# Float16 products, rows turned by DMA and three dense experts in a mixture-of-experts layer behind attention

## What is computed

```python
w, idx = _gate(xf, wg)
fe = idx.reshape(-1)
oh = jax.nn.one_hot(fe, E, dtype=jnp.int32)
pos = (jnp.cumsum(oh, axis=0) * oh).sum(-1) - 1
keep = pos < cap
dest = jnp.where(keep, fe * cap + pos, E * cap)
...
xe = xp[buf_tok].reshape(E, cap, DIM)
h = jax.nn.silu(jnp.einsum('ecd,edh->ech', xe, w1)) * jnp.einsum('ecd,edh->ech', xe, w3)
out = jnp.einsum('ech,ehd->ecd', h, w2) * buf_w.reshape(E, cap, 1)
y = jnp.zeros((N + 1, DIM), x.dtype).at[buf_tok].add(out.reshape(E * cap, DIM))[:N]
z = jax.nn.silu(xf @ sw1) * (xf @ sw3) @ sw2
return (y + z).reshape(shape)
```

## Time and profile before

| | |
|---|---|
| median of 3 runs | 969.25 us (966.09 to 976.89) |
| span of the profiled execution | 977.5 us |
| TensorE, VectorE, ScalarE, GpSimd busy | 859.0, 654.3, 616.8, 673.5 us |
| mean granted clock of TensorE | 0.943 of full speed |

### The profile page before, as it was taken

The page is one execution under the profiler, slowest core; times in us unless marked ns, Lnnn a source line. Parts: engine busy times, 40 slices in busy tenths (PEclk is TensorE's granted clock), DMA queues, the critical chain, the costliest instruction groups (busy, mean ns, idle before and its releaser), DMA issues. The chain is left out here.

```text
span 977.5 us, 25690 instructions
## 1 busy us (share of the span) xinstructions
PE 859.0 (88%) x9439; PEld 633.9 (65%) x9439; DVE 654.3 (67%) x2448; ACT 616.8 (63%) x1189; POOL 673.5 (69%) x580
## 2 busy tenths in 40 slices
PE   5789999999999999999999999766688888888654
PEld 2367777777777777777777777654465666666422
DVE  7757788987987987987987986836243434343217
ACT  3668889888888888888898787733132323233305
POOL 7656665699698699699689689346665555556636
PEclk9989999999999999999999999978798989899968
DMA  5787788645444454354354342016333323333147
GB/s 160 182 255 234 231 243 220 177 107 134 97 119 111 101 135 108 89 151 107 73 141 122 72 117 64 21 51 197 119 96 100 96 79 95 95 101 99 39 191 252
DMA packets 104428, 126.62 MB, mean 130 GB/s; under 512 B 22077, under 2 KB 65426, under 8 KB 103408
## 3 DMA queue, kind: packets, MB, share of 16 engines
q1 hardware_dynamic: 95408, 109.25, 40.8%
q0 software_dynamic: 8896, 15.74, 5.2%
HBM read 33.68 MB, written 41.58 MB: 77 GB/s over the span
## 5 line engine op out<-in xcount | busy, mean ns | idle before, releaser
L2289 POOL TENSOR_TENSOR PL<-PF,PH 128x1280 f16<-128x1280 f32 x121 | 317.8, 2626 | 107.2 <-ACT PH L1632 63.7
L1854 DVE CUSTOM_DVE_ANT_0 JUNK<-PS,M 128x256 f16<-128x256 f32 (+3 forms) x512 | 225.2, 485 | 39.5 <-PE PS L1265 35.8
L1626 ACT ACTIVATE PF<-PS 128x512 f32<-128x512 f32 (+1 forms) x384 | 192.8, 520 | 80.3 <-PE PS L1298 75.4
L2332 POOL DMA_INDIRECT y_rows<-BIG,Q x150 | 145.7, 972 | 99.3 <-ACT BIG L1551 57.4
L1632 ACT ACTIVATE PH<-PF 128x1280 f16<-128x1280 f32 x128 | 162.2, 1267 | 0.6
L2322 POOL DMA_INDIRECT xe_rows<-PAY,DEST x128 | 129.3, 1010 | 42.9 <-issue 27.7
L1291 PE MATMUL PS<-Q,K 128*128 128x512 f16 (+3 forms) x512 | 148.6, 300 | 9.2 <-DMA Q<-MROW 4.9
L1315 PE MATMUL PS<-VH,PH 128*128 128x65 f16 x1280 | 141.3, 195 | 13.0 <-DVE Y L1896 8.5
L1317 PE MATMUL PS<-VH,PL 128*128 128x65 f16 x1280 | 141.3, 194 | 1.2 <-issue 1.2
L1315 PEld LDWEIGHTS PS<-VH,PH 128*128 128x128 f16 x1280 | 119.6, 98 | 35.0 <-issue 24.5
L1316 PE MATMUL PS<-VL,PH 128*128 128x64 f16 x1280 | 141.3, 194 | 0.0
(11 more groups left out here) (252 smaller groups left out, 2027.5 us busy)
## 6 DMA issues: line engine op xcount, KB each, us to landing
K<-KH SPq DMA_DIRECT2D x128, 128.0 KB, 2.3
Q<-QH SPq DMA_DIRECT2D x128, 128.0 KB, 2.4
xe_rows<-PAY SPq DMA_DIRECT2D x20, 520.0 KB, 4.2
Q<-xe_rows SPq DMA_DIRECT2D x30, 325.0 KB
K<-KL SPq DMA_DIRECT2D x64, 128.0 KB, 2.3
Q<-QL SPq DMA_DIRECT2D x64, 128.0 KB, 2.3
y_rows<-PAY SPq DMA_DIRECT2D x16, 512.0 KB, 4.9
K<-in_L_ffn_w_dram SPq DMA_DIRECT2D x96, 64.0 KB
```

The lines of the kernel that those rows point to most:

```text
L1626: e.activation(PF[:, n % PBUF, c0:c0 + width], PS[:, k, 0:width], ACT.Exp).then_inc(s["c_exp"], 1)
L1854: e.tensor_tensor_reduce(JUNK[:, n_ttr % 2, 0:width], PS[:, base + ab, c0:c0 + width], M0[:, 512 - width:512], 1.0, -3e38, ALU.add, ALU.ma ...
L2289: e.tensor_tensor(PL[:, n % PBUF, :], PF[:, n % PBUF, :], PH[:, n % PBUF, :], ALU.subtract).then_inc(s["c_lp"], 1)
L2332: e.indirect_dma_start(out=y4[:, :], out_offset=bass.IndirectOffsetOnAxis(ap=XE[:, x_ % 6, k, 128:129].bitcast(I32), axis=0), in_=OUT[:, x ...
```

## The change

What it does, part by part:

- **Float16 products.** The first layers' operands, rows and weights w1 and w3, are split into a high float16 half (ScalarE) and a low one (VectorE: value less high half), and a product is high x high + high x low + low x high. The second layers stay float32.
- **Rows turned by DMA.** TensorE's turns and their copies go. SyncE issues a DMA transpose of 128 x 1280 float16 for each expert (both halves of its 640 rows) and one of 128 x 1024 for each batch of x1. The stores of the turned x1 to DRAM and their loads go. `xe_rows` is read so that each partition takes five rows that lie 128 apart, not five neighbours.
- **Three dense experts**, four early ones: 29 gathered experts, not 30, and 36 dense pieces (8 shared, 24, 4).
- **TensorE's order**: a front group is the second layer of expert x with the first of x + 2, then a dense group, the second layer of one piece with the first layer of the next; periods 1 to 3 have two dense groups. A group tells the other engines of its end once, behind its last product. Silu and times stand ahead of the five copies.
- Loads of weight sets and of the early experts' rows stand at the end of the attention part in SyncE's order; the last unit's and batch 7's PSUM banks are assigned anew (6 for one half, 7 for the other).

The diff, cut to its core:

```diff
-ND = 2
+ND = 3
 NE = E - ND
-NA = 2
-NS1 = 5
-TAIL = 2
+NA = 4
 SHARED = -1
-DENSE = ([(SHARED, b) for b in range(NS1, NB)] + [(d, b) for d in range(ND) for b in range(NB)]
+DENSE = ([(SHARED, b) for b in range(NB)] + [(d, b) for d in range(ND) for b in range(NB)]
          + [(ND + j, NB - 1) for j in range(NA)])
...
 WEIGHTS = list(range(ND + NA))
...
+SPLITS = [0, SHARED, *range(1, NA + ND)]
...
+    def group(*work):
+
+        told = c["c_pe"].up()
+        for k, (name, a) in enumerate(work):
+            step(name, a, k == len(work) - 1)
+            marks[name, a] = told
+
+    def rows_out(x_):
+        for k in range(5):
+            step("rows out", x_, k)
+
+    begun = []
+
+    def front(*work):
+
+        group(*work)
+        for name, a in reversed(work):
+            if name == "hidden":
+                step("silu", a)
+                step("times", a)
+            else:
+                step("outs", a)
+
+    def dense():
+        nonlocal piece
+
+        work, ended, upped = [], begun[:], None
+        if begun:
+            work.append(("dense down", begun.pop()))
+        if piece < len(DENSE):
+            upped = piece
+            work.append(("dense up", piece))
+            begun.append(piece)
+            piece += 1
+        group(*work)
+        if upped is not None:
+            step("dense silu", upped)
+            step("dense times", upped)
+        for i in ended:
+            step("dense add", i)
...
+        if ms == NH - 3:
+            for j in range(NA + ND):
+                step("load set", j)
+            for x_ in range(NA, NA + 4):
+                step("load ring", x_)
+            for x_ in range(NA):
+                step("load rows", x_)
...
+    rows_in(1)
+    step("set split", SHARED)
+    x1_in(0)
+    piece = 0
+    front(("hidden", 0))
+    step("set split", 1)
+    x1_in(1)
+    rows_in(2)
+    dense()
...
+    front(("product", 0), ("hidden", 1))
+    rows_out(0)
+    step("load rows", 4)
+    step("set split", 2)
+    x1_in(2)
+    rows_in(3)
+    dense()
+    front(("hidden", 2))
+    step("set split", 3)
+    x1_in(3)
+    x1_in(4)
+    dense()
+    splits = SPLITS[5:]
+    forms = list(range(len(WEIGHTS)))
+    for x_ in range(1, NE):
+        rows_in(x_ + 3)
+        if NA <= x_ + 3 < NE:
+            step("ring split", x_ + 3)
+        if x_ + 4 < NE:
+            step("load rows", x_ + 4)
+        if x_ + 2 < NE:
+            front(("product", x_), ("hidden", x_ + 2))
+        else:
+            front(("product", x_))
+        rows_out(x_)
+        if NA + 4 <= x_ + 4 < NE:
+            step("load ring", x_ + 4)
+        dense()
+        for b in (3 + 2 * x_, 4 + 2 * x_):
+            if 5 <= b < NB:
+                x1_in(b)
+        for k in forms[0:2]:
+            step("form", k)
+        forms = forms[2:]
+        for j in splits[0:1]:
+            step("set split", j)
+        splits = splits[1:]
+        if x_ <= 3:
+            dense()
+    while piece < len(DENSE):
+        dense()
+    dense()
+    return steps, marks, {name: x.sem for name, x in c.items()}
...
+        def three(out, halves, m, x_of, free):
+
+            high, low = halves[:, 0, 128 * m:128 * m + 128], halves[:, 1, 128 * m:128 * m + 128]
+            for o, n in free:
+                e.matmul(out(o, n), high, x_of(0, o, n), start=True, stop=False)
+                e.matmul(out(o, n), high, x_of(1, o, n), start=False, stop=False)
+            for o, n in free:
+                i = e.matmul(out(o, n), low, x_of(0, o, n), start=False, stop=True)
+            return i
...
+            three(lambda o, n: PSF[:, o:o + n], halves, 0, rows, ((512, 128),))
+            three(lambda o, n: PSF[:, 896 + o:896 + o + n], halves, 1, rows, ((0, 128),))
+            three(lambda o, n: PSF[:, o:o + n], halves, 0, rows, ((0, 512),))
+            i = three(lambda o, n: PSF[:, 896 + o:896 + o + n], halves, 1, rows, ((128, 512),))
+            if tell:
+                i.then_inc(s["c_pe"], 1)
...
+        def dense_down(i, tell):
+
+            d, b = DENSE[i]
+            if d == SHARED:
+                w.wait_ge(l_sw, 48)
+            else:
+                w.wait_ge(l_set[set_of(d)], 48)
+            w.wait_ge(s_dh, i + 1)
+            w.wait_ge(s_dacc, i)
+            for q in range(4):
+                p = e.matmul(PS[:, 7, q * 128:(q + 1) * 128], DH[:, i % 2, q * 128:(q + 1) * 128], down_weights(d),
+                             start=True, stop=True)
+            if tell:
+                p.then_inc(s["c_pe"], 1)
...
+            elif name == "rows split":
+                x_, = a
+                w.wait_ge(l_xe[x_ % 6], 16 * (x_ // 6 + 1))
+                w.wait_ge(l_xt[(x_ - 2) % 3] if x_ >= 2 else None, 16 * ((x_ - 2) // 3 + 1))
+                for key in unit_done(LAST):
+                    w.wait_ge(*at(*key))
+                e.activation(XS16[:, x_ % 2, 0, :].rearrange("p (k n) -> p k n", k=5), XE[:, x_ % 6, :, 0:128],
+                             ACT.Copy).then_inc(s_rh, 1)
...
+            elif name == "rows split":
+                x_, = a
+                w.wait_ge(s_rh, x_ + 1)
+                w.wait_ge(l_xe[x_ % 6], 16 * (x_ // 6 + 1))
+                w.wait_ge(l_xt[(x_ - 2) % 3] if x_ >= 2 else None, 16 * ((x_ - 2) // 3 + 1))
+                e.tensor_tensor(XS16[:, x_ % 2, 1, :].rearrange("p (k n) -> p k n", k=5), XE[:, x_ % 6, :, 0:128],
+                                XS16[:, x_ % 2, 0, :].rearrange("p (k n) -> p k n", k=5), ALU.subtract).then_inc(s_rl, 1)
...
+        def load_ring(x_):
+            r = x_ - NA
+            if r < 4:
+                for key in unit_done(LAST - 1):
+                    w.wait_ge(*at(*key))
+            else:
+                w.wait_ge(*at("product", x_ - 4))
             for m, src in enumerate((w1, w3, w2)):
-                e.dma_start(EW[:, x_ % 4, m, :], src[expert(x_)]).then_inc(l_w[x_ % 4], 16)
+                e.dma_start(EW[:, r % 4, m, :], src[expert(x_)]).then_inc(l_w[r % 4], 16)
 
         def load_rows(x_):
             b = NB - 1 if x_ >= NA else NB - 2
+            for key in unit_done(LAST - 1 if x_ < 4 else LAST):
+                w.wait_ge(*at(*key))
             w.wait_ge(*at("scat", b, 0))
             w.wait_ge(*at("scat", b, 1))
-            w.wait_ge(s_ys[(x_ - 6) % 4], 80 * ((x_ - 6) // 4 + 1))
-            w.wait_ge(s_turn, x_ - 5)
-            w.wait_ge(s_oc, 5 * (x_ - 5))
+            w.wait_ge(s_ys[(x_ - 6) % 4], 80 * ((x_ - 6) // 4 + 1) if x_ >= 6 else 0)
             e.dma_start(XE[:, x_ % 6, :, :], xe_e[expert(x_)]).then_inc(l_xe[x_ % 6], 16)
...
+            elif name == "rows split":
+                x_, = a
+                w.wait_ge(s_rh, x_ + 1)
+                w.wait_ge(s_rl, x_ + 1)
+                w.wait_ge(*at("pv", NH - 1))
+                w.wait_ge(*at("hidden", x_ - 3))
+                e.dma_start_transpose(XT[:, x_ % 3, :, :].rearrange("p w (k r) -> p (w k) r", r=128),
+                                      XS16[:, x_ % 2, :, :].rearrange("p w n -> p (w n)")).then_inc(l_xt[x_ % 3], 16)
```

More of the change, by code:

```diff
@@ L510, in finish @@
         part("pick", 1)
-        if not whole:
-            unlock((f"pick {half[0]}", b))
         yield
@@ L546, in last_unit @@
         yield
-        step("first out", pj_free[0])
+        step("first out")
         mark("wo", u, "first", by="c_pm")
@@ L562, in last_unit @@
         for half in (0, 1):
-            step("last out", half, (pj_free[1], (("xa", u, "first"),))[half])
+            step("last out", half)
             mark("wo", u, half, by="c_pm")
@@ L773, in plan @@
         scatter()
-    for b in range(NB - 1):
-        load_x1t(b)
-    for e_ in range(4):
-        load_w(e_)
-    step("load dense")
-    for x_ in range(NA):
-        step("load early rows", x_)
-    gate_free = (st_free[0], st_free[1])
     halves = [finish(NB - 1, 0), finish(NB - 1, 1)]
@@ L805, in plan @@
     upto(1, "payi")
-    parts = [shared(b) for b in range(NS1)]
     for half, gen in enumerate(halves):
@@ L813, in plan @@
         if half == 0:
-            next(parts[0])
-            next(parts[1])
+            step("set split", 0)
+            rows_in(0)
     for _ in last:
         pass
-    load_x1t(NB - 1)
-    for b in range(2):
-        next(parts[b])
-    for b in range(2):
-        next(parts[b])
-        next(parts[b])
-    step("early turn", 0)
-    next(parts[2])
-    next(parts[2])
-    step("early hidden", 0)
-    step("early turn", 1)
-    next(parts[3])
-    next(parts[3])
-    step("early product", 0)
@@ L1462, in tensor @@
+            elif name == "hidden":
                 hidden(*a)
-            elif name == "early product":
+            elif name == "product":
                 product(*a)
-        def weights(d, m):
-            return SW[:, m, :] if d == SHARED else DW[:, d, m, :] if d < ND else AW[:, d - ND, m, :]
-        def dense_up(i):
-            d, b = DENSE[i]
-            one, two = (2, 3) if i >= IN_LOOP and i % 2 else (0, 1)
```

(11 more changed lines are left out.)

683 lines of the change are left out of this document (301 added, 382 removed).

## The result

The changed kernel took **988.31 us** (median of 4 runs, 982.30 to 993.46) beside 967.67 for the kernel before (4 runs, 964.04 to 976.89): a ratio of 1.0174, 95% interval 1.0101 to 1.0247. It is 1.7% slower; 922 was predicted. The profiled execution lasted 991.7 us beside before's 977.5; that is 14.2 us between the traces, against 20.6 between the medians, since before's profiled execution lies beside the slowest of its four.

What follows compares the result with a forecast made beforehand. GpSimd waiting behind TensorE bounded the loop; afterwards GpSimd would. Expert 4 at 733.7, last scatter 891.9, loads 894.1, plus 36.3 gives 930.4 instead of 977.5; 47 off the median 969.25 makes 922 us, range 910 to 936.

Steps and rivals of the forecast that it cites:

- GpSimd stood still for 50 us behind TensorE: Expert loop before: 149 scatter steps of 1.276 would be 190.1 us but took 240.6; the difference was winnable.
- TensorE's period of 6.75 us: Old expert loop: turns, dense and expert layers sum to 6.75 us at full clock, 0.37 above GpSimd's 6.38.
- TensorE's new period, 4.99: Expert loop after: float16 first layers 1.62 and 1.26, second layers 1.11 and 1.00, no turns: 4.99 us.
- the loop of buffers: Row load, splits, transpose and first layer take 14 us against three experts' 19.1: five us of slack, hidden.
- the buffer loop is too long: Rival, expert loop: contention makes load and transpose take over 5.1 us more; 15 to 40 us, 937 to 962; chance 0.08.
- GpSimd the bound at 6.38: Expert loop after: five scatters of 1.276 us set 6.38 us an expert, above TensorE's 5.6 at the old clock.
- The start: First experts: GpSimd idles 4 us, three periods of about 10.4 us follow, expert 4's scatters start at 733.7.
- The end: After the last scatter: landing 2.2 us, dense pieces lose 2, earlier sums gain 2; y_rows loads at 894.1.
- scatters slowed by VectorE: Rival, expert loop: VectorE splits with two SBUF inputs hold scatters; 29 us, 951, or half, 937; chance 0.12.
- the row I went by: Earlier trace: scatter at 674.20 beside VectorE's L2078, both inputs in SBUF, still takes 0.97 us; spoke against slowed scatters.
- TensorE at half clock: Rival, expert loop: idle gaps lower TensorE's clock; at 0.50 the period is 10.0 us, total 1,012; chance 0.04.

Runs made afterwards that it cites:

- the first comparison: The changed kernel against the kernel before, without further edits: 988.31 us beside 967.67, ratio 1.0174.
- sets 1, 2 and 4: Follow-up runs, each set on one chip with the kernel before beside it at 974.2, 973.2 and 973.7 us; changed kernel again in set 4: 987.8 us.
- load first: Changed kernel with the load of expert x+4's rows ahead of the splits and transpose of x+3's: 990.2 us, ratio 1.018; in set 5 930.0 us, ratio 1.026.
- set 5: Follow-up runs on another chip, kernel before at 906.05 us: changed kernel 949.1 us, ratio 1.0485; with load first alone 930.0 us.
- set 3: Follow-up runs on another chip, before at 905.68 us: changed kernel with two dense experts, one dense group a period 937.0 us; the same with load first 921.4.
- run 46: Not a run's label: 46 counts scatters that overlap a VectorE operation, in the changed kernel with load first, set 5, 930.0 us.
- spread: Changed kernel with the second dense group of periods 1 to 3 moved to periods 9, 12, 15, 18, 21 and 24: 990.1 us, ratio 1.017.
- layout: Changed kernel reading an expert's rows as the kernel before, five rows in a line to a partition, in pieces of 2,600 bytes: 987.9 us, ratio 1.017.

## Why the prediction was wrong

**"GpSimd stood still for 50 us behind TensorE. That is what the change can win."** This is the step that failed first. GpSimd did wait for work that comes from TensorE, but not for TensorE to do it. On the chips of the first comparison and of sets 1, 2 and 4 a tell arrives up to 9 us late while GpSimd works on indirect DMAs, and 58 us of the kernel before went when its scatters became plain. I had TensorE's period of 6.75 us beside a measured 8.1 and put the gap down to the clock (0.89), although 6.75 / 0.89 is 7.6, so that 0.5 us of each period had no owner, and I didn't ask who the releaser without a name was that stood in ScalarE's waits. Making TensorE's work shorter does nothing to a tell that is late: 8.1 became 7.8. Of the 35.4 us that the loop took over the forecast, 15.8 are gone where no tell is late (193.6 beside 177.8, with nothing changed in the kernel); the other 19.6 come from the loop of buffers and from slowed scatters, below.

**TensorE's new period, 4.99.** Right: 4.9 us in the periods where nothing else holds it (plain DMAs, load first, at a clock of 1.00).

**"Five us of slack: hidden", the loop of buffers.** Wrong, and by its structure. I laid the load, the splits and the transpose over three periods because XE has six slots. The order of SyncE allows one: the load stands behind the transpose of the rows before. The sum of one turn, 6.9 us, is over GpSimd's 6.4; taking it away was worth 19 us (set 5), 15.5 (set 3), 3.7% (plain DMAs), and nothing where late tells cost as much in parallel. The rival "the buffer loop is too long" had the right neighbourhood, with a chance of 0.08, but its condition (5 us more for load and transpose) wasn't the one that decided.

**GpSimd the bound at 6.38.** True only once both are gone: 1.32 us a step in the load-first run on a chip without late tells. On such a chip the kernel before seems to leave this change next to nothing to win; it wasn't traced there, and the sum at the end of this section is the evidence.

**The start.** Expert 4's scatters came at 740.1, not 733.7. The first half of that is a late tell again. The forecast let expert 0's scatters follow at 692.1; they came at 695.24. ScalarE's silu of expert 1 stands ahead of expert 0's copies, and the group that it waits for was over at 690.56 and told at 693.98. Its lines here, then the same instructions on the chip without late tells (set 5):

```profile
690.18 0.38 PE L1198 MATMUL PS<-PL,Q 128*128 128x512 f16 x1
694.00 0.70 ACT L1572 ACTIVATE Y<-PS 128x640 f32<-128x640 f32 x1 [6.17 <-PE PS L1198]
695.24 0.97 POOL L2383 DMA_INDIRECT y_rows<-BIG,Q  x1 [3.23 <-ACT BIG L1583]
695.85 0.45 ACT L1602 ACTIVATE Q<-Q 128x256 f16<-128x256 f32 x1
696.97 0.26 PE L1195 MATMUL PS<-PL,Q 128*128 128x128 f16 x1 [4.22 <-DVE Q L1816]
708.19 0.97 POOL L2383 DMA_INDIRECT y_rows<-BIG,Q  x1 [6.49 <-ACT BIG L1583]
```

```profile
675.75 0.38 PE L1198 MATMUL PS<-PL,Q 128*128 128x512 f16 x1
676.16 0.70 ACT L1572 ACTIVATE Y<-PS 128x640 f32<-128x640 f32 x1 [2.19 <-PE PS L1198]
677.83 0.97 POOL L2383 DMA_INDIRECT y_rows<-BIG,Q  x1 [0.30 <-ACT BIG L1583]
679.13 0.22 PE L1195 MATMUL PS<-PL,Q 128*128 128x128 f16 x1 [0.81 <-ACT Q L1602]
```

There expert 0's scatters do follow at once, as forecast. I had also missed that the split of expert 2's weights (L1602, then L1816) stands behind these copies: TensorE waits 4.2 us for it here, but 0.8 on the other chip, so most of that wait too comes from the late tell. From expert 0's to expert 1's first scatter it takes 12.9 and 12.3 us on the two chips, where I had 10.4; that part of the miss is there without late tells. The periods from there to expert 4 took 10.6 us in the mean, near the 10.4. In all the start takes 44.9 us here and 44.4 there, beside 31.9 before.

**The end.** I allowed 2 us; it cost 17 more than before. The pieces were counted at 4.5 us each (2.26 and 2.2 uncovered); they took 6.2 to 7.2, at a clock of 0.58 and with add, silu and times in a row. TensorE had no lead over GpSimd in which to hide them, since it was not GpSimd that held the loop, and 9.4 us are one late tell. Without late tells the tail is 11.0 us. The kernel before has the same hole, and I read it as its natural end: the stretch 927 to 941 of the earlier trace rows, with TensorE at 0.50. Its second layer L1488 was over at 925.59, told at 934.91, and the add starts on that:

```profile
934.94 1.12 DVE L2163 SCALAR_TENSOR_TENSOR X<-PS,GA,X 128x128 f32<-128x128 f32 x4 [7.05 <-remote]
```

**The rival of the scatters slowed by VectorE.** The mechanism is there, against the row I went by the earlier trace rows. In the turn shown above VectorE's split runs from 816.21 to 817.04, and the scatter that starts at 816.28 takes 1.60 us instead of 0.97; the next one comes 1.92 after it instead of 1.28. The Trainium skill, SBUF — State Buffer, section "SBUF: two separate sides", has a VectorE operation with two SBUF inputs and a GpSimd one that reads SBUF exclude each other; the trace agrees. The size was over-stated: a scatter is 1,013 ns in the mean with the load first, beside 972 before, so 145 of them lose 6 us and not 29. Over all 145 scatters of that run 46 overlap a VectorE operation with both inputs in SBUF by more than 0.1 us; 17 of these take over 1.05 us, and none of the other 99 does. One short operation beside one scatter was too little evidence to rule it out.

**Slower: TensorE at half clock.** Not it: the granted clock in the loop is 0.89, as before, and 0.95 on a chip without late tells.

Where no tell is late, the spans differ by 41.9 us (946.2 beside 904.3). Before has no trace on such a chip, so what follows is an estimate. Suppose that its first scatter starts at 677.8 like the changed kernel's (in the first comparison the two agree, 695.26 and 695.24) and that its 149 steps go at GpSimd's 1.276: that leaves 36.4 us behind the last scatter's start. The shortest tail of any run is 2.1 us, and the kernel before with plain DMAs takes 33.2 from the loads to the end, 35.3 together. So by this estimate before's GpSimd was idle for hardly more than a microsecond there, and the change found nothing to win. Its cost, against this pace: 18.9 us at the start (44.4 beside 4 x 6.38 = 25.5), 19.6 in the loop (177.8 beside 124 x 1.276 = 158.2), 9.9 behind the last scatter (46.3 beside 36.4), less one expert, 6.4; the sum, 42.0, closes by the way it is made. Of the loop's 19.6 the load first takes away 14.4, and slowed scatters are some 3 (145 times 995 less 972 ns).

What stays open: by what path GpSimd's work on an indirect DMA holds back TensorE's semaphore updates, and why two chips don't show it. The pause of 0.14 us was the only remedy tried. Over five traces with late tells (before, after, load first, spread, layout), 65 of the 66 tells that fell due 2.5 us or more after the start of GpSimd's last scatter came on time, so a pause of some 2 us should let them through; at one an expert it would cost as much as it gives, and it wasn't tried.

## What to carry to other kernels

Before the sum of a period is believed, divide the measured period by it: a gap that the granted clock doesn't fill has an owner, and the list of waits names it, even if only as an unknown releaser. Follow an in-order queue step by step when work is moved into it: six buffers give no slack if each load is issued behind the step that consumes the load before. Where two limits are nearly equal, undoing one shows nothing, so an edit without effect is to be tried again with the other limit out of the way.

## What the runs showed of the hardware

In the first comparison and on the chips of sets 1, 2 and 4 TensorE's semaphore updates come up to 9.4 us late while GpSimd works on indirect DMAs, whether or not these write their rows, and on time with plain DMAs of the same size. Held updates come out in bunches, as the four between 843.98 and 844.13. On two other chips none was late with the same instructions. The same kernel takes 906 us there and 967 to 974 elsewhere, 7% more. The stretch ahead of this change is touched too: the first scatter of expert rows starts at 677.8 instead of 695.2, after 128 indirect DMAs of the attention part. A comparison of two kernels of this kind has to be made on one chip: the same change costs 1.6 to 1.7% on one kind and 4.8% on the other.
